# Last edge pass of a four-layer graph network: another order on VectorE and TensorE, marks of each group's first node made once

## The reference

```python
f_src = (feat @ W_src.T + b_src).reshape(n, HEADS, OUT_FEATS)
f_dst = (feat @ W_dst.T + b_dst).reshape(n, HEADS, OUT_FEATS)
f_v = (feat @ W_v.T + b_v).reshape(n, HEADS, OUT_FEATS)
a = f_src[src] + f_dst[dst]
e = jnp.where(a >= 0, a, NEG_SLOPE * a)
sa = _edge_softmax(e, dst, n)      # exp(e - max over the destination) / sum over the destination
m = f_v[src] * sa
rst = jax.ops.segment_sum(m, dst, num_segments=n)
```

## Time and profile before

| | us |
|---|---|
| median of 3 runs (5306.94 to 5311.58) | 5311.27 |
| the profiled execution | 5308.46 |
| its span, first to last instruction | 5306.7 |
| of it the last edge pass, from its first instruction to the last group's scans | about 3846 to 5205 |

### The profile page before, as it was taken

One profiled execution on the slowest core, in us unless ns is written; L12 is line 12 of the kernel. 1 busy time (PEld: TensorE's weight loads), 2 busy tenths in 40 slices (PEclk: granted clock), 3 DMA queues, 4 the chain that ended last, 5 costly groups with the idle time before them and its releaser, 6 DMA issues. The chain is left out here.

```text
span 5306.7 us, 96549 instructions
## 1 busy us (share of the span) xinstructions
PE 3639.6 (69%) x20063; PEld 3004.1 (57%) x20064; DVE 3680.0 (69%) x8656; ACT 2909.3 (55%) x7558; POOL 3627.0 (68%) x3835
## 2 busy tenths in 40 slices
PE   6444444451766666666678888888778888888882
PEld 4444444441655555555466666666567777777771
DVE  5666666667644444445577777777679999999997
ACT  2444444443522222224566666666479998989893
POOL 4777777773777777774477777777067777777772
PEclk7778877775877777777788988898989999999996
DMA  7444444442423333331111111111166666666661
GB/s 193 146 159 153 152 152 152 154 160 68 110 77 78 79 78 78 77 77 39 51 55 55 55 55 55 55 55 55 51 170 175 175 176 174 174 175 173 173 175 36
DMA packets 490311, 596.75 MB, mean 112 GB/s; under 512 B 126676, under 2 KB 348358, under 8 KB 489832
## 3 DMA queue, kind: packets, MB, share of 16 engines
q0 software_dynamic: 141696, 349.47, 23.6%
q1 hardware_dynamic: 347656, 245.85, 16.1%
q10 hardware_dynamic: 864, 0.39, 0.0%
HBM read 505.89 MB, written 30.07 MB: 101 GB/s over the span
## 5 line engine op out<-in xcount | busy, mean ns | idle before, releaser
L893 DVE TENSOR_TENSOR acc<-acc,banks 128x256 f32 (+1 forms) x3520 | 1359.9, 386 | 760.1 <-PE banks L869 500.8
L808 POOL DMA_INDIRECT e_rows<-kv_t,e_index x800 | 785.4, 982 | 243.7 <-issue 242.4
L808 POOL DMA_INDIRECT e_rows<-fsv_t,e_index x800 | 775.6, 970 | 257.8 <-issue 257.8
L808 POOL DMA_INDIRECT e_rows<-x_t,e_index x800 | 778.7, 973 | 249.7 <-issue 239.9
L808 POOL DMA_INDIRECT e_rows<-up_t,e_index x800 | 777.3, 972 | 243.8 <-issue 238.3
L869 PE MATMUL banks<-e_rows,e_sel 128*128 128x256 f32 x3520 | 920.6, 408 | 22.9 <-issue 14.7
L844 ACT ACTIVATE e_away<-node_iota,local 128x128 f32<-128x128 f32 x2640 | 840.3, 389 | 8.0 <-issue 1.0
L869 PE MATMUL banks<-e_msg,e_sel 128*128 128x137 f32 (+1 forms) x3520 | 762.2, 366 | 9.9 <-DVE acc L893 4.5
L869 PEld LDWEIGHTS banks<-e_rows,e_sel 128*128 128x128 f32 x3520 | 683.9, 205 | 136.4 <-issue 38.3
L970 PE MATMUL banks<-acc,e_sel_t 128*128 x1760 | 315.1, 335 | 580.6 <-DVE e_sel_t L937 566.3
L1095 ACT ACTIVATE e_rows<-banks,e_rows 128x128 f32<-128x128 f32 x880 | 250.0, 369 | 800.1 <-PE banks L1086 387.7
(11 more groups left out here) (202 smaller groups left out, 6637.1 us busy)
## 6 DMA issues: line engine op xcount, KB each, us to landing
e_near<-near_d SPq DMA_DIRECT2D x440, 258.0 KB, 4.2
e_far<-acc SPq DMA_DIRECT2D x880, 64.0 KB
e_attr<-in_attr_rows SPq DMA_DIRECT2D x880, 32.0 KB
e_rows<-kv_t,e_index POOLq DMA_INDIRECT x800
e_rows<-x_t,e_index POOLq DMA_INDIRECT x800
e_rows<-up_t,e_index POOLq DMA_INDIRECT x800, 2.5
e_rows<-fsv_t,e_index POOLq DMA_INDIRECT x800
kv_t<-proj_kv SPq DMA_DIRECT2D x12, 512.0 KB, 4.8
```

Of the source, the lines that this page charges most:

```text
L808: G.indirect_dma_start(out=self.rows[:, u, i, 0:self.width], out_offset=None, in_=self.table, in_offset=bass.IndirectOffsetOnAxis(ap=index ...
L893: V.tensor_tensor(to, to, bank[n_bank][:, col:col + self.sums].unsqueeze(1), ALU.add).then_inc(self.s_added[i], 1)
```

## The change

Everything is inside `edges3`.

1. DVE's order within a step. Before: leaky, scaled, add 0, add 1, add 2, message, add 3, forward, backward. After: scaled, at_firsts, add 0, message, add 1, forward, add 2, backward, add 3, leaky. Each member of the chain of adds now has another instruction behind it, and so has the forward scan.
2. PE's order. Before: below_top, spread_resets (lag 3), both_ends, factors, sums_a (item 0), sums_b (items 1 to 3). After: below_top, both_ends, factors, sums_a (items 0 and 1), spread_resets (lag 2), sums_b (items 2 and 3). The resets of the next group are spread once the backward scan of this step is done.
3. ACT loses three instructions of a step: `not_first`, `from_first` and `at_firsts`. The last goes to DVE as one compare-and-multiply. `shrinks` moves from lag 5 to lag 4.
4. The marks `firsts` (each group's first node) and `others` are made once for all 220 groups as the pass begins: a DMA of 220 single numbers, a copy, one matmul that spreads them, and two DVE instructions.
5. The load of `near` waits for `turn`'s first instruction of two groups earlier (s_apart), no longer for `from_first` and `not_first`.

```diff
+            with nc.allow_non_contiguous_dma(reason="one number of each group, once"):
+                SP.dma_start(first_row[:], near_d[0:N_GROUPS, 1:2].rearrange("g a -> a g")).then_inc(s_heads, 16)
+            V.wait_ge(s_heads, 16)
+            V.tensor_copy(first_b[:], first_row[:]).then_inc(start, 1)
+            PE.wait_ge(start, 5)
+            PE.matmul(bank[B_F][:, 0:N_GROUPS], ones_row[:], first_b[:], start=True, stop=True).then_inc(spread_heads, 1)
+            V.wait_ge(spread_heads, 1)
+            V.tensor_scalar(firsts[:], bank[B_F][:, 0:N_GROUPS], 1.0 / STEP, None, ALU.mult).then_inc(start, 1)
+            V.tensor_scalar(others[:], bank[B_F][:, 0:N_GROUPS], node_step[:], None, ALU.not_equal).then_inc(start, 1)
+            V.wait_ge(start, 7)
+            PE.wait_ge(start, 7)
             def gather(g):
-                if g.old(2):
-                    SP.wait_ge(s_others, g.upto(-2))
-                by_node.load(g, s_gap)
+                by_node.load(g, s_apart)
                 ps.gather(g, ps.s_sums[-1])
...
             def at_firsts(g):
-                A.wait_ge(s_gap, g.upto(0))
-                A.wait_ge(s_shrink, g.upto(0))
+                V.wait_ge(s_shrink, g.upto(0))
                 if g.old(2):
-                    A.wait_ge(s_f, g.upto(-2))
-                A.activation(at_first[:, g.r2, :], gap[:, g.at(SPAN), :], ACT.Relu, bias=shrink[:, g.r2:g.r2 + 1],
-                             scale=-1.0).then_inc(s_first, 1)
+                    V.wait_ge(s_f, g.upto(-2))
+                V.tensor_scalar(at_first[:, g.r2, :], node_iota[:], firsts[:, ds(g.n, 1)], shrink[:, g.r2:g.r2 + 1],
+                                ALU.is_equal, ALU.mult).then_inc(s_first, 1)
...
             def scaled(g):
                 V.wait_ge(s_f, g.upto(0))
-                V.wait_ge(s_others, g.upto(0))
...
             def sums_a(g):
+                PE.wait_ge(ps.s_sel, g.upto(0))
                 PE.wait_ge(s_msg_g, g.upto(0))
-                PE.wait_ge(ps.s_sel, g.upto(0))
-                ps.scatter(g, lambda i: [(0, ps.row(g)[:, i, :])], (0,))
+                PE.wait_ge(s_msg_v, g.upto(0))
+                ps.scatter(g, lambda i: [(0, ps.row(g)[:, i, :])], (0, 1))
             def sums_b(g):
-                PE.wait_ge(s_msg_v, g.upto(0))
-                ps.scatter(g, lambda i: [(0, ps.row(g)[:, i, :])], (1, 2, 3))
+                ps.scatter(g, lambda i: [(0, ps.row(g)[:, i, :])], (2, 3))
             ps.run([(0, gather), (0, load_far), (1, load_resets), (5, message(G, s_msg_g, slice(0, 1))),
-                    (4, below_top), (3, spread_resets), (1, both_ends), (5, factors), (5, sums_a), (5, sums_b),
-                    (5, distance), (2, take), (5, shrinks), (0, turn), (0, not_first), (1, from_first), (5, at_firsts),
-                    (5, at_zero), (4, exps),
-                    (2, leaky), (6, scaled), (6, ps.add(0, s_scaled)), (6, ps.add(1)), (6, ps.add(2)),
-                    (5, message(V, s_msg_v, slice(1, 4))), (6, ps.add(3)), (3, forward), (3, backward)])
+                    (4, below_top), (1, both_ends), (5, factors), (5, sums_a), (2, spread_resets), (5, sums_b),
+                    (5, distance), (2, take), (4, shrinks), (0, turn), (5, at_zero), (4, exps),
+                    (6, scaled), (5, at_firsts), (6, ps.add(0, s_scaled)), (5, message(V, s_msg_v, slice(1, 4))),
+                    (6, ps.add(1)), (3, forward), (6, ps.add(2)), (3, backward), (6, ps.add(3)), (2, leaky)])
```

More of the change, by code:

```diff
@@ L1335, in edges3 @@
             top = ps.sb("top", [P, SPAN, EDGES])
-            gap = ps.sb("gap", [P, SPAN, P])
             rise, shrink = ps.sb("rise", [P, 1]), ps.sb("shrink", [P, 2])
             at_first = ps.sb("at_first", [P, 2, P])
-            others = ps.sb("others", [P, ROUND])
+            firsts, others = ps.sb("firsts", [P, N_GROUPS]), ps.sb("others", [P, N_GROUPS])
+            first_row = ps.sb("first_row", [1, N_GROUPS])
+            first_b = ps.sb("first_b", [1, N_GROUPS], BF16)
             minus, minus_node = ps.sb("minus", [P, P]), ps.sb("minus_node", [P, 1])
@@ L1344, in edges3 @@
                 ps.sem(n) for n in ("a", "taken", "l", "r", "run", "top", "d", "exp", "msg_g", "msg_v"))
-            s_apart, s_gap, s_rise, s_shrink, s_first, s_f, s_others, s_scaled, start = (
-                ps.sem(n) for n in ("apart", "gap", "rise", "shrink", "first", "f", "others", "scaled", "start"))
+            s_apart, s_rise, s_shrink, s_first, s_f, s_scaled, start, s_heads, spread_heads = (
+                ps.sem(n) for n in ("apart", "rise", "shrink", "first", "f", "scaled", "start", "heads", "spread_heads"))
             B_A, B_D, B_R, B_F = (2, 3), (4, 5), 6, 7
@@ L1375, in load_resets @@
                 SP.dma_start(resets[:, g.r2, :], reset_d[ds(g.n, 1), :]).then_inc(s_resets[g.r2], 16)
-            def first(g):
-                return by_node.near[:, g.r2, 0, 1:2]
             def turn(g):
@@ L1390, in turn @@
                     A.wait_ge(s_a, g.upto(-2))
-                    A.wait_ge(s_others, g.upto(-2))
                 A.activation(by_node.sel_t[:, g.r2], apart[:], ACT.Relu, bias=ones_col[:], scale=-1.0
                              ).then_inc(by_node.s_t, 1)
[L1395 to L1406, removed]
             def both_ends(g):
@@ L1494, in scaled @@
                 V.scalar_tensor_tensor(out=to, in0=bank[B_F][:, 0:D].unsqueeze(1).to_broadcast([P, 2, D]),
-                                       scalar=others[:, g.at(ROUND):g.at(ROUND) + 1], in1=to, op0=ALU.add, op1=ALU.mult
+                                       scalar=others[:, ds(g.n, 1)], in1=to, op0=ALU.add, op1=ALU.mult
                                        ).then_inc(s_scaled, 1)
```

## The result

The changed kernel takes **5158.73 us** (median of 4 runs, 5153.3 to 5176.94). The kernel before, run beside it, takes 5311.43 us (4 runs, 5306.94 to 5312.59). The ratio is 0.972, with a 95% interval of 0.9695 to 0.9745. The forecast was 5231, with a range of 5190 to 5270: the direction was right, and the gain of 2.8% was nearly double the forecast 1.5%.

What follows compares the result with a forecast made beforehand. DVE's stream was taken as the bound at 6.00 us a step; the new step, the largest of DVE 5.38, PE 5.46 and POOL 5.63, gains 0.41, over 220 steps 90 us, 80 after deductions: 5231 us, range 5190 to 5270.

Steps and rivals of the forecast that it cites:

- The step that failed: On POOL: four gathers and a product, with unexplained gaps that stay, need at least 5.63 us a step, setting the pace.
- The free step of 5.51: On POOL: a single step without a wait, read from the earlier trace as 5.51 us, below the 5.63 used.
- rival (a): On POOL: its gaps shrink and PE becomes the bound at 5.46 us a step, giving 5193 us; chance 0.12.
- PE's floor: On PE: its own matmul work, total less its wait for the backward scan, needs 5.46 us a step.
- the terms for filling, jitter and start: Over the whole pass: deductions from the gain of 3 us for pipeline filling, 6 for jitter, 1 for the start.
- DVE's order: On DVE: separating chained adds and scans, with at_firsts mostly hidden, cuts the step from 6.00 to 5.38 us.
- Rival (c): On DVE: adds cost the same chained or not, so at_firsts adds 0.20 us a step, giving 5346 us; chance 0.05.
- PE's moves: On PE: the wait moves to spread_resets, results still come in time both ways, so the moves cost nothing.
- Rival (d): On PE and DVE: a loop of spread, forward, add 2 and backward holds the step at 6.0, no change; chance 0.04.
- Rival (b): Across three engines: PE waits 0.4 us at spread_resets, 5.85 a step, 5269 us; chance 0.14, including results nearer no change.
- ACT, SP, marks and start: ACT's lost instructions and SP's earlier load pay nothing; DMA's share grows to about 0.69; the start's new chain costs 1 us.

Runs made afterwards that it cites:

- the first series: Changed kernel, kernel before with either order alone, and changed kernel with a DVE clearing, all some 21% slower than elsewhere; ratios to before 1.0051 to 1.0077.
- the second profile: The changed kernel run again with no edit, against the kernel before: 5161.06 us, ratio 0.9706, steps of 5.38 or 5.39 us.
- the clearing: The changed kernel with a clearing of 128x384 numbers added on DVE behind leaky: 5218.5 us, ratio 0.9813 to the kernel before.
- first profile: The profiled execution of the changed kernel's first measurement, slowest of its four: 5176.94 us, steps of 5.49 us.
- phase set: The changed kernel with POOL's product, in groups written out around the loop, also waiting for leaky of two groups on: 5178.77 us, ratio 0.9742.

## Why the prediction was wrong, step by step

**The step that failed** is "all else is its own busy time and unexplained gaps between its instructions, which stay. So its floor is (900 - 61.2)/149 = 5.63". The gaps did not stay. They are long only where POOL waits: before, with either order alone, and in the first series, there behind 149 of 149 waits and 0 of 49 steps without one. In the kernels of before and of either order a gap above 0.16 also stands behind some products without a wait of their own (15 of 32 before), so the wait of a neighbouring step may be enough; that is not shown. In the five profiles in which POOL multiplies and never waits there is no gap but 0.15 to 0.17 and 0.30 to 0.31. What POOL does in the long gaps the traces do not show. That it is work of its sequencer which a run without waits gets done in advance is a guess.

The trace of before held the answer. The free step of 5.51 that I read the earlier trace rows has a gap of 0.30 behind its product; with 0.16, which 17 of the 32 products without a wait had, and 0.02 up to the next product, it is 5.39 (5.51 - 0.14 + 0.02). I took the average over waits for the better number because it held more steps. With POOL at 5.38 the sum would have gone by PE's 5.46 and given 5193, rival (a). Only with PE's floor put right too does it go by 5.38: 0.66 x 220 - 10 = 135 us, 5173 + 3 = 5176. That is below the range, and still 17 us above what was measured. Of these, 10 are the terms for filling, jitter and start, for which the runs show nothing: from first to last forward scan the second profile of the changed kernel takes 1186.5 us (3870.2 to 5056.6), 144.9 less than before, and that is 219 x 0.66 without a deduction.

**DVE's order** was right: 5.38 forecast, 5.38 measured in the second profile, where DVE's product loses nothing. Its terms: unchained adds 0.31 to 0.33 (forecast 0.33 or 0.34), scans 1.19 or 1.20 (1.19), leaky 0.60 (0.59), scaled with at_firsts 0.64 (0.60; bounds from 0 to 0.39 for at_firsts, in fact 0.07). The gain of the whole change is this term, with PE's order to let it through: DVE was the bound before and is the bound now, with POOL's 5.38 beside it.

**Rival (c)** is refuted by the same rows. The rule of the Trainium skill, page "VectorE: DVE Perf Modes", section "The DRAIN you can't avoid", by which operations chained without semaphores take as long as with them, does not hold for these adds: 0.58 to 0.60 behind an own result, 0.31 to 0.33 without, for the same 128x256 numbers. The same section also says that a next operation that is not held starts earlier, which the prediction left out; with that the trace agrees.

**PE** was mis-sized in the same way, and did no harm only because POOL's floor stood above it. Its own step is 5.06, not 5.46; below_top and both_ends take 1.33 each, not 1.48 and 1.39, and factors 0.11, not 0.27. (900 - 86.0)/149 took these longer times for PE's own; why they were longer is not shown. That PE's moves cost nothing is right, but not that they bring nothing: without them DVE's order brings nothing (0.9996). Rival (d) named a loop of resets and scans and added it to 3.3 us. In the new order that holds nothing up; in the old one the sums and below_top stand in the loop too and it adds to 6.02, and I had not priced the old order with DVE's new one.

**Rival (a)** had the mechanism that came, POOL's gaps shrinking, at 0.12. Its price of 5193 hung on PE's 5.46 and was 34 us too high. Rival (b) had PE's wait at the resets right (0.4, measured 0.42), but put it on a floor of 5.46; on 5.06 it is slack, and nobody waits for it.

**ACT, SP, marks and start** came out as priced. ACT's busy time fell from 812.23 to 766.94 us with a tenth more steps. DMA's share is 0.70, forecast 0.69. The new chain at the start is hidden: PE's first matmul of `both_ends` is at 3861.71, against 3861.89 before, though the last instruction of the chain is what releases it. (The first forward scan is earlier, 3866.5 against 3870.9, because leaky of the next group no longer stands before it.) The marks without the new order were not tried.

**What was missing** is the collision of DVE's product with POOL's work. It made the profiled run 5.49 a step and not 5.38, some 18 us of the total; the prediction had 6 us for jitter and no such mechanism. It also ties POOL to DVE where POOL has slack, as without POOL's product and with the clearing.

## What to carry to other kernels

Take an engine's floor from steps in which it waits for nobody, not from the total less its waits: here both floors taken in the second way were too high, by 0.25 and 0.4 us of 5.4. On DVE, put an independent instruction behind each one whose result the next needs, and change the order of the engine that feeds it in the same step, or the gain turns into a wait. Where two engines read SBUF side by side, look at the durations and not only at the waits: an instruction held by the other engine's shows up as a longer one, with no row in the view of waits.

## What the runs showed of the hardware

A DVE product of two SBUF operands and POOL's work slow each other. Beside **POOL's product**, DVE's product of 128x384 loses 0.10 (first profile), 0.14 to 0.15 (phase set) or 0.20 us (at_firsts on ACT). Beside a **gather's issue**, DVE loses nothing, and the gather takes 1.13, 1.24 or 1.33 us instead of 0.95 to 0.99, and 1.39 beside a product of 128x512. The adds and scans on DVE, which have an operand in PSUM, stand beside gathers of 0.95 in every profile.

How long the loser is held follows one line. In the ten profiles outside the first series, every gather that starts more than 0.04 us behind the start of DVE's product and more than 0.13 us ahead of its end, 1,046 in all, ends 0.81 to 0.83 us behind that end (0.86 or 0.87 for the gather right behind POOL's product). Two of them, from the trace of before, DVE's row above POOL's:

```profile
4468.60 0.55 DVE L1519 TENSOR_TENSOR e_rows<-e_rows 128x384 f32<-128x384 f32 x1
4468.65 1.32 POOL L808 DMA_INDIRECT e_rows<-fsv_t,e_index  x1 [0.30 <-issue]
4577.26 0.55 DVE L1519 TENSOR_TENSOR e_rows<-e_rows 128x384 f32<-128x384 f32 x1
4577.48 1.15 POOL L808 DMA_INDIRECT e_rows<-fsv_t,e_index  x1 [0.30 <-issue]
```

So a gather loses what is left of the product less 0.13. A DVE product that starts inside POOL's product loses by the same line: overlaps of 0.26 and 0.33 cost 0.14 and 0.20, and in all 369 with an overlap of more than 0.13 the next instruction starts 0.34 or 0.35 behind the end of POOL's product. This is also why POOL keeps DVE's step without waiting for it: the earlier it comes, the longer it is held.

The Trainium skill's page "SBUF — State Buffer", section "SBUF: two separate sides", says that the two engines share one pair of ports, that a DVE instruction with two SBUF inputs contends for it with a GpSimd instruction that reads SBUF, and that the loser waits for the whole of the other's instruction. The trace agrees for these two cases, but for the constant 0.13. It does not agree in the first profile, where DVE's product started 0.37 to 0.40 ahead of POOL's in nearly every step and both lost, 0.10 and 0.11; why is open.
